# A decoder recurrence with TensorE's order changed: energies ahead of the gate transpose, mask in column tiles

## The reference, cut to what matters

```python
def step(carry, tgt):
    s, c, alpha = carry
    f = lax.conv_general_dilated(alpha, conv_w, (1,), 'SAME', dimension_numbers=('NCH', 'OIH', 'NCH'))
    e = jnp.einsum('a,bta->bt', va, jnp.tanh(enc_proj + (s @ Wa_s.T)[:, None, :] + jnp.einsum('bft,af->bta', f, Wa_f) + ba))
    e = jnp.where(mask, e, jnp.float32(-1e+30))
    alpha_new = jax.nn.softmax(e, axis=1)[:, None, :]
    g = jnp.einsum('bt,btd->bd', alpha_new[:, 0], hbatch)
    y = jnp.tanh(g @ L_gy_w.T + L_gy_b + s @ L_sy.T) @ L_yy_w.T + L_yy_b
    rec = tgt @ L_ys.T + s @ L_ss.T + g @ L_gs_w.T + L_gs_b
    ig, fg, cg, og = jnp.split(rec, 4, axis=1)
    c_next = _sig(fg) * c + _sig(ig) * jnp.tanh(cg)
    s_next = _sig(og) * jnp.tanh(c_next)
    return ((s_next, c_next, alpha_new), y)
```

## Time and profile before

| | |
|---|---|
| median of 3 runs | 4269.8 us (4262.49 to 4271.77) |
| the profiled execution, its own time | 4264.92 us |
| its span, first to last instruction | 4263.1 us |
| stretch of the 255 halves | 2196.1 to 3766.2 us of the span |
| TensorE busy over the span | 3495.4 us (82%) |
| VectorE, ScalarE, GpSimd busy | 2396.7, 1385.3, 504.8 us |

### The profile page before, as it was taken

The page is one execution under the profiler, slowest core; times in us unless marked ns, Lnnn a source line. Parts: engine busy times, 40 slices in busy tenths (PEclk is TensorE's granted clock), DMA queues, the critical chain, the costliest instruction groups (busy, mean ns, idle before and its releaser), DMA issues. The chain is left out here.

```text
span 4263.1 us, 92698 instructions
## 1 busy us (share of the span) xinstructions
PE 3495.4 (82%) x35188; PEld 2095.6 (49%) x35188; DVE 2396.7 (56%) x5626; ACT 1385.3 (32%) x3454; POOL 504.8 (12%) x1854
## 2 busy tenths in 40 slices
PE   6546488444699999995989999999999999964998
PEld 3424155222477666662545555555555555532554
DVE  2665777588555555552135655655655655654444
ACT  2221244345322222221124444444444444422222
POOL 0000511233200000000000000000000000023222
PEclk8666699666799999997999999999999999986888
DMA  2000010200100000001012232232232232211000
GB/s 90 3 3 10 10 36 6 82 0 0 42 1 0 0 0 0 0 0 50 25 52 77 77 80 77 77 80 77 77 80 77 77 80 77 77 33 45 25 25 30
DMA packets 282427, 176.61 MB, mean 41 GB/s; under 512 B 18078, under 2 KB 271528, under 8 KB 282296
## 3 DMA queue, kind: packets, MB, share of 16 engines
q1 hardware_dynamic: 279608, 172.54, 14.4%
q0 software_dynamic: 2752, 3.18, 0.4%
HBM read 164.94 MB, written 13.90 MB: 42 GB/s over the span
## 5 line engine op out<-in xcount | busy, mean ns | idle before, releaser
L1790 PE MATMUL ps<-st_hk,de_wct 112*128 112x512 f32 x1024 | 547.5, 616 | 43.1 <-DMA st_hk<-padded_alignments 30.5
L1814 PEld LDWEIGHTS ps<-de_hg,st_at 128*32 128x32 f32 x16384 | 431.9, 110 | 193.8 <-DVE st_at L1952 193.0
L1814 PE MATMUL ps<-de_hg,st_at 128*32 128x128 f32 x16384 | 500.9, 274 | 0.3 <-DVE st_at L1952 0.3
L1867 ACT ACTIVATE st_th<-ps,st_sw 128x128 f32<-128x128 f32 x1024 | 292.8, 368 | 315.1 <-DVE st_sw L1926 315.1
L1931 DVE COPY ps<-de_enc 128x512 f32<-128x512 f32 x512 | 351.3, 687 | 6.1 <-PE ps L1847 6.1
L1770 POOL COPY de_ah<-st_at 128x8 f32 (+1 forms) x256 | 50.9, 199 | 1708.3 <-DVE st_at L1952 1708.3
L1247 PEld LDWEIGHTS ps<-sa_xt,w_wq 128*128 128x128 f32 x2048 | 234.4, 193 | 11.6 <-issue 9.7
L1247 PE MATMUL ps<-sa_xt,w_wq 128*128 128x128 f32 x2048 | 237.7, 277 | 2.4 <-DVE sa_ident L1460 1.3
L1318 PE MATMUL ps<-sa_wo,sa_ct 128*128 128x512 f32 x512 | 226.4, 601 | 13.1 <-issue 13.1
L1942 DVE TENSOR_REDUCE st_nm<-ps 128x1 f32<-128x128 f32 x256 | 74.7, 292 | 268.2 <-PE ps L1800 268.2
L1800 PE MATMUL ps<-st_th,st_vas 128*32 128x128 f32 x4096 | 218.1, 285 | 1.0 <-ACT st_th L1867 0.9
(11 more groups left out here) (406 smaller groups left out, 6112.7 us busy)
## 6 DMA issues: line engine op xcount, KB each, us to landing
st_hk<-padded_alignments SPq DMA_DIRECT2D x508, 224.0 KB, 3.3
X<-in_x_dram SPq DMA_DIRECT2D x16, 512.0 KB, 11.9
out_dram<-X SPq DMA_DIRECT2D x16, 512.0 KB, 2.7
w_wq<-in_Wq_perm_dram SPq DMA_DIRECT2D x1, 4096.0 KB, 17.7
sa_wo<-in_Wo_perm_dram SPq DMA_DIRECT2D x1, 4096.0 KB, 14.6
gate_inputs<-dp_ro SPq DMA_DIRECT2D x16, 256.0 KB, 2.3
st_rin<-gate_inputs SPq DMA_DIRECT2D x128, 32.0 KB, 3.0
rf_wf<-in_weightT_dram SPq DMA_DIRECT2D x8, 512.0 KB, 4.4
```

The costliest lines, as they stand in the source:

```text
L1790: pe.matmul(CV[g][i], wct[:, :], hk[g][:, 4 * i:4 * i + 4, :].rearrange("p b n -> p (b n)"), start=False, stop=True, skip_group_check=True ...
L1814: ins = pe.matmul(R[g][32 * q:32 * q + 32, :], at[g][:, b, :], hg[:, BG * g + b, q * P:(q + 1) * P], start=False, stop=(b == BG - 1), tile ...
L1867: ins = act.activation(th[g][:, b, :], CV[g][0][:, b * P:(b + 1) * P], ACT.Tanh, bias=sw[g][:, b:b + 1])
```

## The change

Four things on TensorE, and nothing on another engine:

- `mask` is four bf16 matmuls in column tiles (128x32 stationary, 32 rows out each) in place of one over the whole array.
- `gates_of_context` is cut in two halves of 16 matmuls, and `mask(o, m)` stands between them.
- `energy(o, m, 0)` and `energy(o, m, 1)` both come right after it, ahead of `turn_gates(g, n)`.
- `gates_of_state(o, m)` is last in the half, after `turn_gates(g, n)`.

```diff
--- before.py
+++ after.py
@@ -1792,7 +1792,9 @@
 
                     def mask(g, n):
                         pe.wait_ge(sw_ready[g], n + 1)
-                        pe.matmul(E[g], ident16[:, :], mask16[:, g, :], start=True, stop=False, skip_group_check=True)
+                        for j in range(4):
+                            pe.matmul(E[g][32 * j:32 * j + 32, :], ident16[:, 32 * j:32 * j + 32], mask16[:, g, :],
+                                      start=True, stop=False, tile_position=(0, 32 * j), skip_group_check=True)
 
                     def energy(g, n, i):
                         pe.wait_ge(th_done[g], 2 * n + i + 1)
@@ -1807,13 +1809,14 @@
                             pe.matmul(R[g][32 * q:32 * q + 32, :], sT[g][:, :], lss[:, q * P:(q + 1) * P],
                                       start=True, stop=False, tile_position=(0, 32 * q), skip_group_check=True)
 
-                    def gates_of_context(g, n):
+                    def gates_of_context(g, n, h):
                         pe.wait_ge(at_ready[g], n + 1)
-                        for b in range(BG):
+                        for b in range(4 * h, 4 * h + 4):
                             for q in range(4):
                                 ins = pe.matmul(R[g][32 * q:32 * q + 32, :], at[g][:, b, :], hg[:, BG * g + b, q * P:(q + 1) * P],
                                                 start=False, stop=(b == BG - 1), tile_position=(0, 32 * q), skip_group_check=True)
-                        ins.then_inc(r_sum[g], 1)
+                        if h == 1:
+                            ins.then_inc(r_sum[g], 1)
 
                     def turn_gates(g, n):
                         pe.wait_ge(rec_ready[g], n + 1)
@@ -1831,14 +1834,16 @@
                         turn_alignment(g, n)
                         if front:
                             convolve(o, m, 1)
-                        gates_of_context(g, n)
+                        gates_of_context(g, n, 0)
+                        if front:
+                            mask(o, m)
+                        gates_of_context(g, n, 1)
+                        if front:
+                            energy(o, m, 0)
+                            energy(o, m, 1)
+                        turn_gates(g, n)
                         if front:
                             gates_of_state(o, m)
-                            mask(o, m)
-                            energy(o, m, 0)
-                        turn_gates(g, n)
-                        if front:
-                            energy(o, m, 1)
 
                     pe.wait_ge(w_load, 80)
                     pe.wait_ge(set_up, SETUP)
```

## The result

The changed kernel takes 4389.5 us (median of 4 runs, 4372.46 to 4395.88) against 4270.8 for the kernel before on the same chip: a ratio of 1.0276 (95% interval 1.0245 to 1.0307), slower by 119 us. Forecast were 4132 us. Neither the amount nor the sign was right.

What follows compares the result with a forecast made beforehand. The one-half TensorE chain (6.15 us) was taken as the bound, then the two-half loop through memory: 5.63 per half from 6.157, 0.53 times 255 = 135 us saved, 4132 us; own range 4115 to 4150 (64%), wider 4095 to 4180.

Steps and rivals of the forecast that it cites:

- Mask in the context: Four bf16 column-tile matmuls amid the context products add 0.11 us, with no drain for the change of type.
- Energies: The 16 energy instructions run right behind the context products and end at S+3.83, 0.82 us earlier than before.
- Transpose: TensorE's transpose of the gates starts at S+3.82, before 3.97, released by VectorE's `rec`.
- Tail: From maximum to state: exp waits for the end of `gt`, S+4.38, 0.66 us earlier; alignment ends at S+5.36.
- Gates of state hidden: Moved behind the transpose, they end before the first convolution's start at S+4.7, with 0.2 us to spare.
- The trip: Way through memory from the end of a group's alignment to its first convolution: 4.95 us; state term 0.94 behind.
- the two-half loop: Alignment through memory to convolution and state term: 5.36 + 4.95 + 0.94 = 11.25 us, 5.63 per half.
- the DMA is not the bound: Rival, 8%: trips through memory take 4.7 us, so the one-half chain of 5.49 decides; 4095 us.
- step 1: The mask's four column tiles amid the context products, priced at 0.11 us from the neighbouring loads' 26.4 ns each.
- only the order of the work matters: Premise for TensorE in the recurrence: it has its full clock there, 1.00, its level of 2.4 GHz.
- its own signs of being wrong: Mask run over 0.3, transpose past S+4.0, mean trip outside 4.85 to 5.1, clock below 1.00, half near 5.49.
- slower: Rival, 4%: DMA trips stretch beyond 6.01 us as halves shrink, each 0.1 costing 13 us; 6.3 gives 4302.

## Why the prediction was wrong

What each step said, and what the changed kernel showed where it doesn't stall. One half of the one with the two-step loop, which has the same order; S is 2800.58. TensorE:

```profile
2799.65 1.10 PE L1790 MATMUL ps<-st_hk,de_wct 112*128 112x512 f32 x2 [0.42 <-DMA st_hk<-padded_alignments]
2800.58 0.29 PE L1785 MATMUL ps<-st_sT,st_was 128*128 128x8 f32 x2
...
2801.82 0.81 PEld L1816 LDWEIGHTS ps<-de_hg,st_at 128*32 128x32 f32 x32 [0.76 <-DVE st_at L1957]
...
2802.61 0.12 PEld L1796 LDWEIGHTS ps<-st_mask,st_ident 128*32 128x32 bf16 x4
2802.72 0.84 PEld L1816 LDWEIGHTS ps<-de_hg,st_at 128*32 128x32 f32 x32
2803.65 0.62 PE L1802 MATMUL ps<-st_th,st_vas 128*32 128x128 f32 x16
2804.24 0.14 PEld L1823 LDWEIGHTS ps<-identity,st_rec 128*128 128x128 f32 x1 [0.25 <-DVE st_rec L1974]
...
2805.01 0.30 PEld L1790 LDWEIGHTS ps<-st_hk,de_wct 112*128 112x128 f32 x2 [0.35 <-DMA st_hk<-padded_alignments]
```

VectorE and ScalarE in the same half:

```profile
2804.34 0.29 DVE L1947 TENSOR_REDUCE st_nm<-ps 128x1 f32<-128x128 f32 x1
...
2804.61 0.20 ACT L1887 ACTIVATE st_gt<-ps 128x32 f32<-128x32 f32 x1 [1.33 <-PE ps L1823]
2804.70 0.36 ACT L1880 ACTIVATE st_ex<-ps,st_nm 128x128 f32<-128x128 f32 x1
...
2805.39 0.28 DVE L1952 TENSOR_SCALAR st_al<-st_ex,st_ri 128x128 f32<-128x128 f32 x1
```

- *Mask in the context*, 0.11: right, 2802.61 to 2802.72, without an idle time on either side. The change of type inside a tiled stream, of which no row of before told anything, costs no drain here; the full-array mask in the same place has its 0.20.
- *Energies* end at S+3.83: they end at 2804.27, S+3.69, 0.10 of the difference because the context starts at S+1.24 (2801.82) and not at S+1.34: the state term takes 0.29 and no longer 0.39. Why it does was not tested.
- *Transpose* at S+3.82: S+3.66, released by `rec`, as said.
- *Tail.* exp at S+4.38, behind the end of `gt`: it starts at S+4.12, 0.09 after `gt` starts; ScalarE overlaps the two. The alignment ends at S+5.09 in place of S+5.36. The term from `gt` to exp was 0.1 too long by itself; the rest of the 0.27 is the earlier transpose.
- *Gates of state hidden*: right; the convolution behind them waits for its DMA.
- *The trip*, 4.95, and 0.94 behind it: 4.91, and 2800.58 - 2799.65 = 0.93. So the two-half loop is 5.09 + 4.91 + 0.93 = 10.93 or 5.47 for a half; measured are 5.51, forecast were 5.63.

The sum of these steps forecast 4132; the same order without the stalls measured 4099.6 (4105.8 with the four-step loop moved on), under the 4115 at which the forecast's own range began, the difference being mostly the tail's term for exp and the context's start. It lies close to the 4095 of the rival "the DMA is not the bound", but by accident: that rival wanted trips of 4.7, they were 4.91, and the swapped loads show that the loop through memory is still the bound. So the chain of the recurrence was understood up to 0.12 us in a half, and the kernel on the chip was slower for a reason that no step and no rival had: step 1 priced the mask's tiles by their time, 0.11 us, and not by their instructions. Six more in a half, 48 in the loop, were enough to move its end over the edge of a block, and 30 times TensorE stood 4.3 us and then ran slow. The sentence at which it failed is that "only the order of the work matters" in this stretch; getting the loop's instructions to TensorE stood in the sum at nothing. Of its own signs of being wrong, the granted clock below 1.00 came, 0.93. (4389.5 - 4099.6)/30 = 9.7 us for each branch back. By the means of the eight halves, against 5.51 each, 5.3 of them fall in the long half (4.3 are the idle time itself), 1.4 in the next and 3.0 in the six others. The lower clock lasts for 6.7 us and more behind the idle time of the pass shown above, and trips that were put off start late in the next halves; how the rest of the 9.7 divides between these two was not tested. The rival "slower" had the sign by a mechanism that did not happen: the trips of the changed kernel do read longer (median 5.31 over the 224 that did not end at a stall), but they are back at 4.9 as soon as the stalls are gone, so they follow from the stalls.

What stays open is why the loop that ended some 20 instructions past the edge was read again at 13 of 30 branches in one execution and, going by their times, seldom or never in others, and what TensorE waits for once the second packet has landed.

The fastest kernel run is the changed order with the two-step loop, 4099.6 us, 3.8% under the kernel before.

## What to carry to other kernels

Count the instructions of a hardware loop on TensorE, not only their time: in this kernel 1585 ran without being read again in three places and were partly read again in a fourth, 1633 were read again in one place and not in another, and the 819 of two steps ran without it at no cost. If a change slows a loop, look at the packets of the instruction queue and at idle time that recurs once per pass with "issue" as its releaser before doubting the order. A change that adds a few small instructions to a long loop should be timed with a shorter loop as well, or a gain of 4% can be read as a loss of 3%.

## What the runs showed of the hardware

- A branch back that stalls is followed by nine packets of 16.4 KB on the instruction queue, two at the idle time and seven over the pass, and costs 4.3 us of idle TensorE, then a convolution of 2.07 us for 1.12 at a granted clock of 0.50; 9.7 us in all in the changed kernel, 8.4 in the order of before.
- The kernel before ended its loop just ahead of an edge: 24 instructions put once in front of it made single executions up to 110 us longer. Two executions of the one moved by 52, whose start stands at the other edge, were also 53 and 71 us over its median.
- Four bf16 tiles between f32 tiles part the loads of the context by 0.09 us; one full-array matmul in the same place by 0.36.
- ScalarE started exp 0.09 us after a small tanh of 0.20 us that it had begun, when both inputs were there.
